# An adaptive FFN with routed adapters on one core: another order for the first two token groups (y_lo ahead of the next x, x_hi products ahead of x_lo, x loaded before the router and adapter weights)

## What is computed

```python
q_emb = relu(cond @ W3 + b3)                      # 64 x 512
v     = (n * x + sum(x, axis=1)) * q_emb          # n = 64 tokens of a batch
y     = relu(v @ W2 + b2)                         # "m1": 512 -> 512
base  = y @ W_base + b_base                       # "m2": 512 -> 512
shared = (y @ A_s) @ B_s                          # rank 16
gates = softmax(y @ W_router + b_router)          # 6 experts, the best 2 are kept
h     = y @ A_r                                   # 6 experts x rank 16
out   = x + base + shared + (h * w_per_expert) @ B_r
```

## Time and profile before

| | |
|---|---|
| time, median of 3 runs | 237.69 us (237.68 to 237.79) |
| the profiled execution's own time | 237.04 us |
| its span, first to last instruction | 235.2 us |
| TensorE busy | 229.3 us, 97% |
| VectorE, ScalarE, GpSimd busy | 71%, 37%, 21% |
| granted TensorE clock | 1.000 in all of the span |
| loads and stores | 28.80 MB, mean 122 GB/s |

### The profile page before, as it was taken

One profiled execution on the slowest core, in us unless ns is written; L12 is line 12 of the kernel. 1 busy time (PEld: TensorE's weight loads), 2 busy tenths in 40 slices (PEclk: granted clock), 3 DMA queues, 4 the chain that ended last, 5 costly groups with the idle time before them and its releaser, 6 DMA issues.

```text
span 235.2 us, 3088 instructions
## 1 busy us (share of the span) xinstructions
PE 229.3 (97%) x1006; PEld 186.9 (79%) x1006; DVE 166.7 (71%) x309; ACT 86.2 (37%) x171; POOL 49.0 (21%) x57
## 2 busy tenths in 40 slices
PE   7999899999999999999999999999999999999994
PEld 3977687788888888888888888888888888888883
DVE  0794997798979967497838969299665976064344
ACT  3369451534136330444206340263305351252330
POOL 6288422012132211023012120022111130000000
PEclk9999999999999999999999999999999999999999
DMA  6999903527053632717044541709020370104004
GB/s 214 340 219 227 253 4 71 142 99 261 11 137 65 222 137 37 175 70 289 8 117 89 187 172 22 185 4 329 28 33 0 126 231 13 22 0 178 3 0 178
DMA packets 32505, 28.80 MB, mean 122 GB/s; under 512 B 5817, under 2 KB 22909, under 8 KB 32494
## 3 DMA queue, kind: packets, MB, share of 16 engines
q1 hardware_dynamic: 30682, 28.50, 42.4%
q10 hardware_dynamic: 1812, 0.17, 0.6%
HBM read 18.89 MB, written 8.39 MB: 116 GB/s over the span
## 4 chain that ended last, share of the span: by engine, by line
PE 87%; SPq 6%; DVE 2%; DMA 2%; issue 0%; DVEq 0%
PE m_ps L747 78%; PE hT L747 9%; SPq L210 3%; DMA x_quart<-in_x_dram 2%; DVE out_nat L625 1%; SPq L226 1%; SPq L233 1%; SPq L229 1%; DVE xT L471 0%; SPq L231 0%; DVE vsum L476 0%; DVE x_sum L483 0%; SPq L237 0%; DVE y_lo L497 0%; SPq L236 0%
## 5 line engine op out<-in xcount | busy, mean ns | idle before, releaser
L308 POOL TENSOR_TENSOR x_full<-x_sum,qT 128x512 f32<-128x512 f32 x28 | 32.4, 1156 | 136.7 <-DVE x_sum L483 136.7
L353 ACT ACTIVATE y_hi<-m_ps,condT 128x512 fp32r<-128x512 f32 x32 | 21.9, 686 | 80.4 <-PE m_ps L747 80.2
L747 PE MATMUL m_ps<-Wb_lo,y_hi 128*128 128x512 f32 x128 | 49.8, 389 | 0.0
L747 PE MATMUL m_ps<-Wb_hi,y_hi 128*128 128x512 f32 x128 | 49.8, 389 | 0.0
L747 PE MATMUL m_ps<-Wb_hi,y_lo 128*128 128x512 f32 x128 | 49.8, 389 | 0.0
L747 PE MATMUL m_ps<-x_hi,W_hi 128*128 128x512 f32 x112 | 43.8, 391 | 0.0
L747 PE MATMUL m_ps<-x_hi,W_lo 128*128 128x512 f32 x112 | 43.6, 389 | 0.0
L747 PE MATMUL m_ps<-x_lo,W_hi 128*128 128x512 f32 x112 | 43.6, 389 | 0.0
L497 DVE TENSOR_TENSOR y_lo<-m_ps,y_hi 128x512 fp32r<-128x512 f32 x32 | 21.7, 677 | 30.3 <-ACT m_ps L355 30.3
L471 DVE STREAM_TRANSPOSE xT<-x_quart 128x512 f32<-128x512 f32 x28 | 30.3, 1084 | 3.0 <-DMA x_quart<-in_x_dram 3.0
L747 PEld LDWEIGHTS m_ps<-Wb_hi,y_lo 128*128 128x128 f32 x128 | 24.0, 188 | 5.0
(11 more groups left out here) (99 smaller groups left out, 255.1 us busy)
## 6 DMA issues: line engine op xcount, KB each, us to landing
out_dram<-out_nat SPq DMA_DIRECT2D x32, 256.0 KB, 2.3
x_quart<-in_x_dram SPq DMA_DIRECT2D x28, 256.0 KB, 4.5
x_nat<-in_x_dram SPq DMA_DIRECT2D x7, 1024.0 KB, 6.2
gatesT<-wT SPq DMA_DIRECT2D x28, 48.0 KB
x_nat<-in_x_dram SPq DMA_DIRECT2D x4, 256.0 KB, 3.4
W_f<-in_L_cond_W_dram SPq DMA_DIRECT2D x4, 256.0 KB, 6.0
Wb_f<-in_L_ffn_W_base_dram SPq DMA_DIRECT2D x1, 1024.0 KB, 8.7
W_sb<-in_L_cond_W_dram SPq DMA_DIRECT2D x2, 256.0 KB, 4.2
```

Source lines behind the costliest of these rows:

```text
L308: nc.gpsimd.tensor_tensor(per_batch(x1_full[:, c, :]), per_batch(x1_sum[:, c, :]), qT[:, c, bass.ds(BG * g, BG)].unsqueeze(2).to_broadcast ...
L353: nc.scalar.activation(y_hi[:, m, :], m1_ps[m][:, :], ACT.Relu, bias=b2_sb[:, m:m + 1]).then_inc(y_hi_ready, 1)
L747: mm = nc.tensor.matmul(psum, lhsT, rhs, start=start and i == 0, stop=stop and i == len(terms) - 1)
```

## The change

Only groups 0 and 1 and the loads before them are touched. Names in the pieces of order below end in a buffer's number.

- **Loads (SyncE).** The four quarters of group 1's x move ahead of the router's, the shared adapter's and two of the routed adapters' loads into `Wd_f`.
- **Wd (ScalarE, GpSimd).** `Wd_hi` moves from between the splits of x and W2 to behind the relu of y's first tile; `Wd_lo` moves behind the first two `Wb_lo`.
- **Head.** One idle matmul fewer (WARM_HALF 2 to 1). ScalarE takes a relu of q ahead of each step it stood behind before. TensorE does chunk 0 of `m1_first` for tiles 0 to 2 first, tile 3 after them, then the `x_lo` products.
- **Group 0, VectorE.** `y_lo` of tile 0 comes before the first transpose; the third chunk of the next x moves behind the gates, and all four `x1_lo` to the end.
- **Group 1, TensorE.** `m1_second` does for tiles 0 to 2 all products with `x_hi`, chunk by chunk, and then those with `x_lo`, tile by tile.
- **Group 1, VectorE and ScalarE.** The gated h and its parts come before y's first tile. `pick_round`, needed by the last group alone, moves here from group 0.

```diff
--- before.py
+++ after.py
@@ -46,7 +46,7 @@
     SH = 16
     RO = 32
 
-    WARM_LOAD, WARM_W3, WARM_HALF, WARM_Q = 7, 1, 2, 1
+    WARM_LOAD, WARM_W3, WARM_HALF, WARM_Q = 7, 1, 1, 1
     assert ONE < SH and SH + R <= RO and RO + E * R == P and TT == KC and NG % 2 == 0 and NG >= 4
 
     x_groups = x.rearrange("b n d -> (b n) d").rearrange("(g t p) d -> g p t d", t=TT, p=P)
@@ -232,11 +232,11 @@
             for c in range(KC):
                 sp.dma_start(W2_f[:, c, :], W2.rearrange("(p c) n -> p c n", c=KC)[:, c, :]).then_inc(W2_loaded[c], 16)
             sp.dma_start(Wb_f[:, :, :], W_base.rearrange("(k p) d -> p k d", p=P)).then_inc(Wb_loaded, 16)
+            load_quarters(1, 1)
             sp.wait_ge(zeroed, 3)
             sp.dma_start(Wd_f[:, :, 0:E], W_router.rearrange("(k p) e -> p k e", p=P)).then_inc(Wd_loaded, 16)
             sp.dma_start(Wd_f[:, :, SH:SH + R], A_s.rearrange("(k p) r -> p k r", p=P)).then_inc(Wd_loaded, 16)
             load_A_r(sp, range(KC // 2, KC))
-            load_quarters(1, 1)
             sp.wait_ge(zeroed, 4)
             sp.dma_start(Wu_f[ONE:ONE + 1, :], b_base.rearrange("(a d) -> a d", a=1)).then_inc(Wu_loaded, 16)
             sp.dma_start(Wu_f[SH:SH + R, :], B_s).then_inc(Wu_loaded, 16)
@@ -316,9 +316,10 @@
             for c in range(KC):
                 pool.wait_ge(W2_hi_ready, c + 1)
                 W_rest(W2_lo[:, c, :], W2_f[:, c, :], W2_hi[:, c, :], W2_lo_ready)
-            pool.wait_ge(Wd_hi_ready, 1)
-            W_rest(Wd_lo[:, :, :], Wd_f[:, :, :], Wd_hi[:, :, :], Wd_lo_ready)
             for k in range(KC):
+                if k == 2:
+                    pool.wait_ge(Wd_hi_ready, 1)
+                    W_rest(Wd_lo[:, :, :], Wd_f[:, :, :], Wd_hi[:, :, :], Wd_lo_ready)
                 pool.wait_ge(Wb_hi_ready, k + 1)
                 W_rest(Wb_lo[:, k, :], Wb_f[:, k, :], Wb_hi[:, k, :], Wb_lo_ready)
             scale(1, 0)
@@ -378,18 +379,16 @@
                 nc.scalar.activation(x1_hi[0][:, c, :], head_ps[c][:, :], ACT.Copy).then_inc(x1_hi_ready, 1)
 
             q_relu(0)
+            q_relu(1)
             W2_split(0)
-            q_relu(1)
+            q_relu(2)
             x1_split_head(0)
-            q_relu(2)
+            q_relu(3)
             x1_split_head(1)
-            q_relu(3)
             W2_split(1)
             W2_split(2)
             x1_split_head(2)
             W2_split(3)
-            act.wait_ge(Wd_loaded, 16 * (2 + KC))
-            nc.scalar.activation(Wd_hi[:, :, :], Wd_f[:, :, :], ACT.Copy).then_inc(Wd_hi_ready, 1)
             x1_split_head(3)
             act.wait_ge(Wb_loaded, 16)
             for k in range(KC):
@@ -423,15 +422,22 @@
                     if not last:
                         x1_split(g + 1, 1 - par, c)
 
+                if second:
+                    hw_split(slice(0, TG), g)
                 for m in range(KC):
                     relu(g, m, first)
-                    if m == 0 and not first:
+                    if m == 0 and first:
+                        act.wait_ge(Wd_loaded, 16 * (2 + KC))
+                        nc.scalar.activation(Wd_hi[:, :, :], Wd_f[:, :, :], ACT.Copy).then_inc(Wd_hi_ready, 1)
+                    if m == 0 and not first and not second:
                         hw_split(slice(0, TG), g)
                     if not first and m >= (2 if second else 1):
                         split(m - (2 if second else 1))
                 if first:
                     act.wait_ge(Wu_loaded, 48)
                     nc.scalar.activation(Wu_hi[:, :], Wu_f[:, :], ACT.Copy).then_inc(Wu_hi_ready, 1)
+                    split(0)
+                if second:
                     pick_round()
 
                 act.wait_ge(h_done, g + 1)
@@ -443,7 +449,6 @@
                 if last:
                     nc.scalar.activation(h_sb[:, :], hT[:, :], ACT.Identity, bias=h_bias[:, 0:1]).then_inc(h_ready, 1)
                 if first:
-                    split(0)
                     split(1)
                 if second:
                     split(2)
@@ -648,23 +653,20 @@
                     hw_rest(slice(0, TG), g)
 
                 if first:
+                    y_rest(g, 0)
+                    turn(0)
+                    y_rest(g, 1)
+                    total(0)
+                    y_rest(g, 2)
+                    turn(1)
+                    y_rest(g, 3)
+                    total(1)
+                elif second:
+                    weigh_before()
+                    hw_rest_before()
+                    y_rest(g, 0)
                     turn(0)
                     total(0)
-                    y_rest(g, 0)
-                    turn(1)
-                    y_rest(g, 1)
-                    sum_x(g + 1, 1)
-                    y_rest(g, 2)
-                    add_sum(g + 1, 1)
-                    y_rest(g, 3)
-                    turn(2)
-                    total(2)
-                elif second:
-                    y_rest(g, 0)
-                    weigh_before()
-                    turn(0)
-                    total(0)
-                    hw_rest_before()
                     y_rest(g, 1)
                     turn(1)
                     add_x(g - 1, 1 - par, UP_TILES[:1], 0)
@@ -698,11 +700,13 @@
                 rank_experts(g)
                 gates(g, last)
                 if first:
-                    rest(0)
+                    turn(2)
+                    total(2)
                 if first or second:
                     turn(3)
                     total(3)
                 if first:
+                    rest(0)
                     rest(1)
                 rest(2)
                 rest(3)
@@ -775,12 +779,24 @@
                                             start=k == 0 and W is W2_hi and x1 is x1_hi,
                                             stop=k == KC - 1 and x1 is x1_lo)
 
-                for k in range(KC // 2):
+                pe.wait_ge(x1_hi_ready, 1)
+                pe.wait_ge(W2_hi_ready, 1)
+                for m in range(KC - 1):
+                    pe.wait_ge(qT_ready, m + 1)
+                    chunk(m, 0, W2_hi, x1_hi)
+                pe.wait_ge(W2_lo_ready, 1)
+                for m in range(KC - 1):
+                    chunk(m, 0, W2_lo, x1_hi)
+                pe.wait_ge(qT_ready, KC)
+                chunk(KC - 1, 0, W2_hi, x1_hi)
+                chunk(KC - 1, 0, W2_lo, x1_hi)
+                pe.wait_ge(x1_lo_ready, 1)
+                for m in range(KC):
+                    chunk(m, 0, W2_hi, x1_lo)
+                for k in range(1, KC // 2):
                     pe.wait_ge(x1_hi_ready, k + 1)
                     pe.wait_ge(W2_hi_ready, k + 1)
                     for m in range(KC):
-                        if k == 0:
-                            pe.wait_ge(qT_ready, m + 1)
                         chunk(m, k, W2_hi, x1_hi)
                     pe.wait_ge(W2_lo_ready, k + 1)
                     for m in range(KC):
@@ -800,6 +816,23 @@
                             if k == KC - 1:
                                 last.then_inc(m1_done, 1)
 
+            def m1_second():
+
+                x_hi, x_lo = x1_hi[1], x1_lo[1]
+                for k in range(KC):
+                    pe.wait_ge(x1_hi_ready, KC + k + 1)
+                    for m in range(KC - 1):
+                        cols = slice(m * P, (m + 1) * P)
+                        product(m1_ps[m][:, :], [(W2_hi[:, k, cols], x_hi[:, k, :]),
+                                                 (W2_lo[:, k, cols], x_hi[:, k, :])], k == 0, False)
+                for m in range(KC - 1):
+                    cols = slice(m * P, (m + 1) * P)
+                    for k in range(KC):
+                        if m == 0:
+                            pe.wait_ge(x1_lo_ready, KC + k + 1)
+                        mm = product(m1_ps[m][:, :], [(W2_hi[:, k, cols], x_lo[:, k, :])], False, k == KC - 1)
+                    mm.then_inc(m1_done, 1)
+
             def h(g, k, first):
 
                 if k == 0 and first:
@@ -858,7 +891,9 @@
                 if first:
                     m1_first()
                 else:
-                    for m in range(KC - 1):
+                    if second:
+                        m1_second()
+                    for m in () if second else range(KC - 1):
                         m1(g, par, m)
                     up(UP_TILES, g)
                     m1(g, par, KC - 1)
```

## The result

| | before | after |
|---|---|---|
| median of four runs | 237.69 us (236.98 to 237.79) | **240.61 us** (240.53 to 241.99) |
| ratio | | 1.0142, 95% interval 1.0111 to 1.0173 |
| the profiled execution's own time, its span | 237.04, 235.2 us | 240.62, 238.8 us |

The change costs 2.9 us. The direction was forecast, but the time lies above the range. From h of group 0 on the stretches on TensorE have the lengths that were forecast. But h began at 25.86 where 22.93 was forecast, 2.9 us late, and that happened in the head.

The account below looks back on a forecast made before the run. TensorE, always busy at full clock late on, bounds the kernel, so only its earlier waits count. Head +0.24, Wd +0.24, y_lo -1.70, group 1's x -0.39, 0.17 gone, new stop +2.44: +0.66, giving 238.3 us, range 236.2 to 239.2.

Parts of the forecast that it names:

- The step that failed: Head: one idle matmul less lets q come about 0.2 us earlier on TensorE.
- Head, order of ScalarE: Head: a second relu of q delays chunk 0's x_hi by 0.14 us, plus 0.10 for the stop: +0.24 us.
- Wd: Before group 0's h: Wd_hi behind tile 0's relu makes Wd_lo late, +0.24 us; loads land at 20.1, covered.
- Wd lands late: Rival: x ahead in the queue makes Wd land at 22.2 instead of 20.1, costing 1.5 us: 239.8 us, chance 0.13.
- y_lo: Group 0's h: no y_lo is late any more, so the wait's 1.70 us are gone.
- Group 1's x: Start of group 1: the 0.39 us of waits for x_hi and x_lo go.
- The stop at the bank: Group 1's m1: tile 3 waits for the bank that VectorE's add_x empties, a new stop of +2.44 us.
- From h to tile 3: Groups 0 and 1: the new stop before m1's tile 3 takes back all that was won.
- the forecast's own range: Whole kernel: the forecast case of 238.3 us spans 237.9 to 238.8 us, chance 0.48.
- The clock falls: Rival: behind group 1's 2.4 us stop, twelve matmuls at 1.2 GHz take 2.7 us more: 241.0 us, chance 0.04.

Follow-up runs that it names:

- a_warm2_2: The changed kernel with the second idle matmul put back (WARM_HALF 2), the same program as a_warm2 measured once more: median 239.52 us.
- a_warm2: The changed kernel with the second idle matmul put back (WARM_HALF 2): 239.57 us (238.27 to 240.34).
- again: The changed kernel run once more, unedited: 241.4 us (240.48 to 242.34).
- a_addx: The changed kernel with VectorE's add_x of the first bank right behind y_lo of tile 0 in group 1: 240.32 us (239.34 to 241.15).
- b_warm1: The kernel before with one idle matmul fewer (WARM_HALF 1), nothing else: 237.78 us, ratio 1.0012.
- b_loads: The kernel before with only the change's early load of x and its moves of Wd_hi and Wd_lo: 237.75 us, ratio 0.9996.
- a_load9_warm2: The changed kernel with nine idle matmuls instead of seven at the start and the second one in q back: 240.84 us.
- b_w3: The kernel before with five more idle matmuls (1.1 us) ahead of q, a pure delay: 238.28 us, ratio 1.001.

## Why the prediction was wrong

**The step that failed** is the first sentence of the head: "One idle matmul less lets q come about 0.2 us earlier". It was costed as time of TensorE alone, and the 0.2 us did come (13.33 with the matmul, 13.12 without). But where it stood the clock stayed up, and without it the clock fell. A second term was put at nothing: what varies ahead of h. While y_lo waited for x, that was covered; the change takes the wait away and the sum had no term for what comes to light. Four profiled executions, all with the bank stop, and that of the kernel before take this apart:

| | rise | clock at the head | m1 starts | tile 3 of group 1 | between | time |
|---|---|---|---|---|---|---|
| a_warm2_2 | early | full | 12.08 | 50.38 | 38.30 | 238.10 |
| a_warm2 | late | full | 13.33 | 51.62 | 38.29 | 239.57 |
| again | early | falls | 11.67 | 51.31 | 39.64 | 240.79 |
| the change | late | falls | 13.12 | 52.78 | 39.66 | 240.62 |
| kernel before | early | full | 11.25 | 49.33 | 38.08 | 237.04 |

The fall of the clock costs 39.65 - 38.30 = 1.35 us between m1's start and tile 3. The late rise costs 13.33 - 12.08 = 1.25 ahead of it, or 13.12 - 11.67 = 1.45 by the other pair; both are differences of single executions. 238.10 + 1.35 + 1.25 - 0.21 for the idle matmul = 240.49, and the changed kernel's profiled execution took 240.62. In the third row the time is 189.48 behind tile 3, where it is 187.7 to 188.0 in the others: 1.6 us for the second fall, behind the stop. In the medians the idle matmul is worth 1.0 us only; with it back they are 239.57 and 239.52, still above the range. That rest is the second term, the late rise in half of the executions or more and at times a fall behind the stop. Whether the change itself makes the rise late is open: no profile with the old loads shows a late rise, so none shows one under the cover of the kernel before either.

How far the fall belongs to the idle matmul: at the head it fell in all four profiles without it (the change, again, a_addx, b_warm1), and in none of the sixteen with it, the kernel before among them. All eight timed executions of the change had a mean clock of 0.993 or less, the same as one fall of 3.4 us or more (half of 3.4 in 238 is 0.007); of the 21 with the matmul put back four had. In b_warm1 it was 4 of 10, so it doesn't fall each time; and in the kernel before, with both idle matmuls, one of the 109 executions measured beside these runs had 0.993 or less, and so had three of the 53 of b_loads and its variants, one of them with 0.986. So two don't rule a fall out.

**The other steps.**
- *Head, order of ScalarE:* forecast +0.24. From the last idle matmul to m1's start it is 11.25 - 10.19 = 1.06 in the kernel before and 13.12 - 11.81 = 1.31 in the change, the same 1.31 in a_warm2_2. So +0.25, at the first matmul already and not only at x_lo of chunk 0, where a_warm2_2 does wait (0.4 us by the waits view) as the kernel before did for q. Less the 0.21 for the idle matmul the term is +0.04: right in its cause, 0.2 too large. In a_warm2_2 m1 starts 0.83 later than in the kernel before; the other 0.58 lies ahead of the last idle matmul (10.77 against 10.19), in transposes and q, and no run ties it to the change.
- *Wd:* forecast +0.24, measured 0.10 + 0.11. Wd_hi follows the relu of tile 0 by 0.57 us, as forecast, with no wait for loads. But that was luck. The loads landed at 22.26, not at 20.1, and were waited for by nobody since the relu of tile 0 came at 23.23, not at 20.2. Had the head been in time, Wd_hi would have been wanted at 20.75, so that by the forecast's own frame the landing of 22.26 would cost 1.5 us (an estimate). In the 14 profiles with the new loads the landing lies from 20.59 to 22.41, all later than 20.1. The rival "Wd lands late" did not come true, but its landing of 22.2 was nearer than the forecast's.
- *y_lo:* -1.70 as forecast; no stop between 26.43 and 39.60 (the 60 matmuls from 25.86 take 13.74 where 13.62 would do, and 0.11 of that is the handover at h).
- *Group 1's x:* the 0.39 are gone, as forecast.
- *The stop at the bank:* forecast 2.44 with its handover, measured 2.28 + 0.11 = 2.39.
- *From h to tile 3* before it is 49.33 - 22.55 = 26.78 us and in the change 52.78 - 25.86 = 26.92. So gain and stop do cancel, as written. With an early rise and a full clock the same program takes 238.10, against 237.7 forecast for the profiled execution; seven of a_warm2's 21 executions lie from 237.9 to 238.8, the forecast's own range.
- *"The clock falls" (0.04):* the mechanism was named, behind the stop, but the place that decided was not. In the profile of the change the clock stayed at 1.00 behind the stop of 2.28 us; in again and in a_load9_warm2 it fell behind the same stop. By the Trainium skill (TensorE: Matmul & The Clock Gate, What's actually happening), an engine that was left idle long enough loses half its clock, and when it changes differs from run to run. The runs agree with the second: the same stop is followed by a fall in one execution and not in another. Of the first they show that the stop alone doesn't decide it; and the fall at the head came with TensorE 96% busy (12 to 13 us), so not behind idle time.

The prediction took the full clock of the kernel before as given for the head of the changed one. It hung on the order of the work there, and on an instruction whose result nobody uses. And it set the median 0.65 us above the profiled execution, as in the kernel before; in the change the two are 0.01 apart.

## What to carry to other kernels

An idle matmul that keeps TensorE busy is not simply time won when it goes: look at what the matmuls behind it would cost at the lower clock. If loads are moved ahead of others, ask when those others land, also when the profile shows no wait for them. Before a wait is removed, ask what else it covers; here it hid most of a delay of 1.6 to 1.8 us at the head (b_w3, b_warm1), and an edit that is measured at nothing under such a cover (b_warm1) cost 1.0 us without it (a_warm2 against the change). And when work is moved out of an engine's way, look where its idle time was: the transposes belonged in VectorE's gap ahead of the gates.

## What the runs showed of the hardware

- The clock column doesn't show the late rise: it reads 1.00 while one transpose takes 0.42 us in one execution and 0.28 in another. The durations of equal instructions tell it.
- The rise changes between executions of the same program: long transposes in the profile of a_warm2, short ones in that of a_warm2_2. Where nothing covers the head, the times lie in two heaps some 1.3 us apart, and a fall adds to the upper one. That is more than the 0.2% that a measurement here was said to tell, so here a change of this size needs ten executions or more, compared heap by heap.
- At the head the clock fell in the four profiles with one idle matmul of 512 columns in the middle of q's 64-column products, in the change behind a us in which TensorE was 96% busy (12 to 13 us); with two there it stayed up in all sixteen.
- Behind a stop of 2.3 us the clock stayed up in five profiles and fell in two.
- Four loads of x put ahead of Wd's in the queue moved Wd's landing from 15.6 to 16.3 us (six profiles) to 20.6 to 22.4 us (14 profiles).
